# The order in which SyncE issues the loads of the first eight experts

## The reference

```python
logits = x @ wg.T
w_topk, idx_topk = jax.lax.top_k(softmax(logits), 8)     # 64 experts, 8 for each token
buf[se, rank] = x[st]                                    # 160 slots for each expert
h = einsum('ech,efh->ecf', buf, expert_w1)               # 256 -> 2 * 768
x1, x2 = jnp.split(h, 2, axis=-1)
out = einsum('ecf,ehf->ech', x1 * silu(x2), expert_w2)   # 768 -> 256
combined = zeros.at[st].add(out[se, rank] * w)           # back to the tokens
x + gb * (shared(x) + combined)
```

## Time and profile before

| | us |
|---|---|
| median of 3 runs | 1852.41 |
| lowest and highest | 1851.78, 1852.84 |
| the profiled execution's own time | 1851.57 |
| its span, first to last instruction | 1849.8 |
| busy PE in the span | 1802.1 (97%) |
| busy POOL, DVE | 922.2, 1206.5 |
| mean granted TensorE clock | 0.991 of full |

### The profile page before, as it was taken

One profiled execution on the slowest core, in us unless ns is written; L12 is line 12 of the kernel. 1 busy time (PEld: TensorE's weight loads), 2 busy tenths in 40 slices (PEclk: granted clock), 3 DMA queues, 4 the chain that ended last, 5 costly groups with the idle time before them and its releaser, 6 DMA issues.

```text
span 1849.8 us, 36105 instructions
## 1 busy us (share of the span) xinstructions
PE 1802.1 (97%) x12362; PEld 1588.7 (86%) x12362; DVE 1206.5 (65%) x2289; ACT 955.1 (52%) x1854; POOL 922.2 (50%) x665
## 2 busy tenths in 40 slices
PE   7999999999999999999999999999999999999995
PEld 5788888888888888787888877899999999999994
DVE  8777777777777776666777668745555555555552
ACT  6666666666666664635444354343444434444341
POOL 5666566665666664035666666664233323333224
PEclk9999999999999999999999999999999999999998
DMA  6211111111111100311111103168898888888883
GB/s 232 69 39 39 35 38 35 38 35 38 35 55 35 38 32 26 124 55 35 46 47 47 40 6 99 46 226 266 285 286 288 285 274 285 287 294 284 267 294 77
DMA packets 141011, 234.04 MB, mean 127 GB/s; under 512 B 24756, under 2 KB 88971, under 8 KB 140816
## 3 DMA queue, kind: packets, MB, share of 16 engines
q1 hardware_dynamic: 116368, 220.50, 34.5%
q0 software_dynamic: 24576, 12.69, 4.5%
HBM read 194.58 MB, written 78.45 MB: 148 GB/s over the span
## 4 chain that ended last, share of the span: by engine, by line
PE 55%; DMA 2%; DVE 1%; issue 1%; POOL 1%; ACT 0%; POOLq 0%; DVEq 0%; ACTq 0%
PE bank L86 26%; PE bank L1942 23%; PE bank L1206 4%; DMA out_rows<-c_y_rest,c_token_rest 2%; PE bank L2164 1%; DMA c_w<-in_e1T 1%; PE bank L1705 1%; POOL out_rows L2116 1%; PE bank L2175 0%; DVE c_y_rest L2083 0%; DVE early L1584 0%; POOLq L2250 0%; PE bank L2169 0%; DVE b_stats L1621 0%; DVE b_swaT L1634 0%
## 5 line engine op out<-in xcount | busy, mean ns | idle before, releaser
L1942 PE MATMUL bank<-c_xT,c_w 128*128 128x160 f32 x3072 | 429.6, 299 | 3.0 <-DMA c_w<-in_e1T 2.4
L1942 PEld LDWEIGHTS bank<-c_xT,c_w 128*128 128x128 f32 x3072 | 419.3, 190 | 4.1 <-DMA c_w<-in_e1T 3.0
L1901 POOL DMA_INDIRECT slots<-b_row,b_index x224 | 251.1, 1121 | 192.3 <-issue 114.1
L2116 POOL DMA_INDIRECT out_rows<-c_y,c_x x64 | 100.3, 1568 | 375.6 <-DMA out_rows<-c_y_rest,c_token_rest 277.5
L2064 DVE TENSOR_TENSOR c_gT<-bank,c_sil 128x480 f32<-128x480 f32 x128 | 84.2, 658 | 211.1 <-PE bank L1942 211.1
L2032 ACT CAST c_gTs_high<-c_gT 128x384 fp32r<-128x384 f32 x128 | 65.6, 513 | 135.4 <-DVE c_gT L2064 135.4
L2025 ACT ACTIVATE c_sil<-bank 128x480 f32<-128x480 f32 x128 | 73.0, 570 | 109.8 <-PE bank L1942 109.3
L2057 DVE TENSOR_TENSOR c_gTs_low<-c_gT,c_gTs_high 128x384 fp32r<-128x384 f32 x128 | 71.5, 559 | 74.8 <-ACT c_gTs_high L2032 74.2
L469 POOL TENSOR_TENSOR last_row<-last_row,a_e 128x256 f32<-128x256 f32 x33 | 54.4, 1647 | 126.4 <-DVE a_e L737 124.7
L86 PE MATMUL bank<-c_w2s_high,c_gTs_high 128*128 128x256 f32 x384 | 114.1, 297 | 0.9 <-DVE c_gTs_low L2057 0.9
L86 PE MATMUL bank<-c_w2s_high,c_gTs_low 128*128 128x256 f32 x384 | 107.0, 279 | 0.0
(11 more groups left out here) (338 smaller groups left out, 5415.1 us busy)
## 6 DMA issues: line engine op xcount, KB each, us to landing
c_w<-in_e1T SPq DMA_DIRECT2D x64, 1536.0 KB, 6.8
c_w<-in_e2T SPq DMA_DIRECT2D x48, 768.0 KB, 8.8
early<-in_e2T SPq DMA_DIRECT2D x16, 768.0 KB, 8.8
slots<-a_fill SPq DMA_DIRECT2D x16, 642.0 KB
c_x<-slots SPq DMA_DIRECT2D x64, 160.5 KB, 8.5
a_x_in<-in_x SPq DMA_DIRECT2D x32, 128.0 KB, 2.0
xT_tiles<-a_xT SPq DMA_DIRECT2D x32, 128.0 KB, 1.7
swaT_tiles<-a_swaT SPq DMA_DIRECT2D x32, 128.0 KB, 1.7
```

Of the source, the lines that this page charges most:

```text
L1901: pool.indirect_dma_start(out=T["slots"], out_offset=bass.IndirectOffsetOnAxis(ap=index[:, t, k:k + 1], axis=0), in_=row[:, t, :], in_offs ...
L1942: return nc.tensor.matmul(out, lhsT, rhs, start=first, stop=last, skip_group_check=True)
L2116: pool.indirect_dma_start(out=T["out"], out_offset=bass.IndirectOffsetOnAxis(ap=token, axis=0), in_=rows, in_offset=None, bounds_check=las ...
```

## The change

In the first eight steps, for expert 2 and on, the wait for `h_mm` and the load of w1 move from behind the loads of rows to the head of the step, ahead of the wait for the level. The load of w2 stays behind the loads of rows. Steps 0 and 1 and the steps from 8 on stay as they are.

```diff
         def step(n, q, i):
             first = isinstance(n, int) and n < RING
+            if first and n >= 2:
+
+                sp.wait_ge(S("h_mm"), (n - 1) * 4)
+                load_w1(sp, n, q % 2)
             if first:
                 sp.wait_ge(B(f"level{n}"), 16 * TPC)
                 if n >= HELD:
...
             wait_past(sp, S("added"), (n - RING + 1) * 32)
             sp.dma_start(x[q][:], slot_rows(T, n, 0, P)).then_inc(S(f"x_in{q}"), 16)
             sp.dma_start(token_rest[q][:], slot_rows(T, n, P, REST)[:, D + E - 1:ROW]).then_inc(S(f"token_in{q}"), 16)
-            if not first or n >= 2:
+            if not first:
 
                 sp.wait_ge(S("h_mm"), (n - 1) * 4)
                 load_w1(sp, n, q % 2)
```

## The result

The changed kernel takes 1873.81 us (median of 6 runs, 1871.07 to 1881.51) against 1852.89 us for the kernel before (6 runs): a ratio of 1.0115, with a 95% interval of 1.0099 to 1.0132. It is slower by 20.9 us, where 11.6 us had been forecast and 17.6 us was the end of the range. The profiled execution took 1876.14 us, 2.3 us above its median.

The account below looks back on a forecast made before the run. PE was taken to bound the kernel, without slack from expert 8 on. New waits for x of 14.6 us less 3.0 us of w1 waits gave +11.6 us on 1852.4, so 1864.0 us; range for 8 in 10, 1856.5 to 1870.

Parts of the forecast that it names:

- What bounds the kernel; the loop has no slack: Whole kernel: PE, busy 97%, sets the time; shifts from the first eight experts are not made good later.
- The gain, 3.0 us: Experts 2 and 3: issuing w1 earlier removes PE's two waits for it, 3.0 us by the weight loads.
- x waits behind w1, 14.6 us: Experts 2 to 7: x lands 0.5 us behind w1 on SP's queue, so PE waits 14.6 us at its transposes.
- Rival 1: Experts 2 to 7: x is served beside w1 or needed later; only the gain is left, 1849.4 us; chance 0.11.
- Rival 2: Early w1 delays the scatters SP waits for; 2 us more per affected expert, 1870.0 us with three; chance 0.10.
- Rival 3: x waits at only one or two experts, 3 us against 3 us, a net of zero, about 1852; chance 0.04.
- Rival 4: Six PE gaps in 60 us lower the granted clock, giving 1875 us or more; chance 0.02.

Follow-up runs that it names:

- fill_4: Changed kernel, with four unused PE products ahead of the wait for x at experts 2, 3, 4, 6 and 7: 1864.54 us, ratio 1.0081.
- gap_before: Kernel before, loads untouched; PE waits for eight ACT copies ahead of the transposes of experts 2, 3, 4, 6 and 7: 1867.79 us, ratio 1.0076.
- two: Changed kernel, with the new order for experts 2 and 3 alone; 4 to 7 keep the old order: 1860.16 us, ratio 1.0038.
- w2_early: Kernel before, order of w1 and rows untouched, but w2 of experts 2 and 3 loaded in step 1: 1850.47 us, ratio 0.9985.
- act_w1: Changed kernel, but ACT issues w1 of experts 2 to 7 on its own queue; SP no longer waits for `h_mm` ahead of rows: 1858.10 us, ratio 1.0033.
- rows_first: Changed kernel, but in steps 2 to 7 only the `h_mm` wait is at the head, w1 behind the row loads: 1852.66 us, ratio 1.0002.
- w2_too: Changed kernel, with w2 also ahead of the level wait and row loads in steps 2 to 7: 1895.68 us, ratio 1.0244.

## Why the prediction was wrong, point by point

- **What bounds the kernel; the loop has no slack.** Right. fill_4, gap_before, two and w2_early carry their shift from expert 12 to 63 with a change of at most 0.2 us. The changed kernel itself lost 3.6 us more in the loop of the profiled execution, which the prediction ruled out ("nothing more is added").
- **The gain, 3.0 us.** Right in place, and in size as far as can be told: no wait for w1 is left in the first eight experts, and with PE's 2.4 us the trace adds up to 20.0 us up to expert 8 (13.9 - 2.4 + 8.5), with 3.0 to 19.4, where 20.2 was measured.
- **x waits behind w1, 14.6 us.** Right, 13.9, but in part by luck. By expert from 2 to 7 forecast 2.3, 3.2, 2.8, 0.7, 3.3, 2.3; measured 2.33, 2.18, 1.87, 0.70, 3.29, 3.56. At experts 3, 4 and 6 w1 took 6.8, 6.6 and 6.9 us, less than the 7.5 to 7.9 assumed for the scatters beside it, and at expert 7 8.3 instead of 7.0. x came 0.5 to 0.7 us behind w1 at experts 3, 4, 5 and 7, as assumed, but 1.6 us at expert 6, which hides the shorter w1 there. The errors cancel. That x was held by the queue, as the prediction has it, fits all these rows; at expert 7 of act_w1 x was as late without w1 in its queue, so the rows do not prove it.
- **Rival 1, x comes through** (the prediction once calls it the second). Ruled out: x took 6.3 to 7.9 us at five experts, and rows_first and w2_too show that it goes by the bytes ahead of it.
- **Rival 2, the levels come late as well.** True at one expert, 2: SP waited until 1217.02 for level 2, where the old order had issued even w1 at 1215.71. x landed 1.1 us behind w1 (1220.7 against 1219.6) instead of the 0.5 us assumed; and as act_w1 shows, at this expert the early w1 makes PE wait even if x doesn't queue behind it. That the gap was still 2.33 us, with 2.3 forecast, is luck: w1 took 6.6 us instead of 7.0.
- **Rival 3, waits at one or two experts only.** Ruled out: all six waited.
- **Rival 4, the clock: the step that failed.** It said: "The 1.69 us gap left it at 1.00 in 1225 to 1235, so I give it 0.02, and 1875 or more." One gap that the clock survived was taken as proof against five longer ones, and the row that it rests on ends 1.1 us behind that gap (the clock stays at 1.00 up to 1240, so the reading was true, but at experts 4 and 6 of the changed kernel the fall came 1.3 us behind the gap). The sum had no term for the clock at all, and the runs show one of 8.5 us, five stretches of 1.7, three quarters of the whole net sum. The price named for the rival was near; its chance and the missing term were wrong. fill_4 takes that part away and lands at 1864.5; gap_before brings it into the old kernel. With the five stretches the sum would have been 11.6 + 5 x 1.7 = 20.1, or 1872.5, against 1873.8.

What stays open is when exactly the clock falls. Gaps of 2.4 us brought it down at four places of gap_before and not at the fifth, one of 1.52 us did in act_w1, those of 1.69 us before and of 1.58 us in fill_4 did not. Nor is it known why the half clock lasted 6.8 us at the gaps of 3.06 us (two) and 3.08 us (act_w1), but 3.4 us at those of 3.29 and 3.56 us in the changed kernel. Open too is why POOL's adds lagged for so long in the profiled execution of the changed kernel (SP's waits for them came to 37.6 us at 9 experts in the same stretch of fill_4, and to 17.1 before), and why its runs spread over 10 us. The clock alone does not explain such a spread: the run of fill_4 that took 1876.03 had the same mean granted clock, 0.989, as the one that took 1864.48.

## What to carry to other kernels

In these runs a small load that followed a large one on the same queue came out 0.5 to 1.6 us behind it, however little it needed by itself: before a large load goes ahead of a small one, compare who needs which first, not which is ready to be issued. A second queue is no sure way round it. Whoever predicts a new gap of the tensor engine has to price it twice, once as idle time and once for the products behind it at half clock; here a gap of 2 us mostly cost nearly 4. And when a load is late because other traffic runs beside it, look first for a load that can go earlier, into idle time, before changing the order in the crowd.

## What the runs showed of the hardware that was not expected

- After the five gaps of 1.9 to 3.6 us of PE in the changed kernel the granted clock was 0.50 for about 3.4 us; after the one of 0.70 us it was not. At gaps of 3.06 us (two) and 3.08 us (act_w1) it was 0.50 for 6.8 us, beginning before the gap was over.
- The same engine kept at work with useless products through the gap kept its clock at 1.00, and the kernel with 17 us of useless work ran 7 to 8 us faster than the one that waited.
- With the six w1 loads on a second hardware queue, beside row and w2 loads on the first, they were slower, 9.2 us in the median instead of 6.9, and one x load with no w1 in its queue still took 6.6 us (act_w1, expert 7).
- A w1 load issued 0.9 us after the last scatter of level 2 made that scatter land 2.4 us later (4.8 to 5.1 us after its issue in six versions, 2.5 us in the four without), on either queue.
